# Ranks and edge lookups for the later chunks made during the first aggregation instead of the second, in a four-layer graph network on one core

## The reference

```python
def _sage_conv(x, src, dst, Wl, Wr, b):
    agg = jax.ops.segment_sum(x[src], dst, num_segments=n)
    deg = jax.ops.segment_sum(jnp.ones_like(dst, dtype=x.dtype), dst, num_segments=n)
    mean = agg / jnp.maximum(deg, 1.0)[:, None]
    return mean @ Wl + x @ Wr + b
...
h = jnp.maximum(_layernorm(x, axis=-1), 0.0)
h = relu(_sage_conv(h, ..., 1)); h = relu(_sage_conv(h, ..., 2)); h = relu(_sage_conv(h, ..., 3))
return x + _sage_conv(h, ..., 4)
```

## Time and profile before

| what | us |
|---|---|
| median of 3 runs | 749.73 (749.73 to 757.46) |
| profiled execution: its own time | 750.45 |
| profiled execution: span from first to last instruction | 748.7 |
| PE busy within the span | 675.0 (90%) |
| DVE busy | 289.1 (39%) |
| ACT busy | 172.8 (23%) |
| POOL busy | 31.3 (4%) |

### The profile page before, as it was taken

One profiled execution on the slowest core, in us unless ns is written; L12 is line 12 of the kernel. 1 busy time (PEld: TensorE's weight loads), 2 busy tenths in 40 slices (PEclk: granted clock), 3 DMA queues, 4 the chain that ended last, 5 costly groups with the idle time before them and its releaser, 6 DMA issues.

```text
span 748.7 us, 11542 instructions
## 1 busy us (share of the span) xinstructions
PE 675.0 (90%) x4545; PEld 367.8 (49%) x4546; DVE 289.1 (39%) x826; ACT 172.8 (23%) x339; POOL 31.3 (4%) x80
## 2 busy tenths in 40 slices
PE   5567867799999999999968999899999999999997
PEld 4234533566555555654434444444444646466464
DVE  6985864468477585840111222202221101001001
ACT  4755521345262361311100101102111000000000
POOL 3000030000000000000000000000000110110100
PEclk9998988979999999999989999999999999999999
DMA  8000200310010101034342334223325330230230
GB/s 259 13 1 1 88 1 31 127 33 5 9 50 16 56 16 32 27 17 57 116 127 80 100 111 153 93 67 114 112 108 208 102 106 12 86 99 3 95 98 28
DMA packets 39424, 53.50 MB, mean 71 GB/s; under 512 B 8557, under 2 KB 21518, under 8 KB 39376
## 3 DMA queue, kind: packets, MB, share of 16 engines
q1 hardware_dynamic: 39260, 52.59, 22.9%
q10 hardware_dynamic: 116, 0.24, 0.1%
HBM read 31.86 MB, written 20.97 MB: 71 GB/s over the span
## 4 chain that ended last, share of the span: by engine, by line
PE 80%; DVE 9%; ACT 3%; DMA 3%; issue 2%; POOL 1%; SPq 1%; DVEq 0%; ACTq 0%; POOLq 0%
PE agg_ps L1673 37%; PE window_ps L1673 12%; PE lin_ps L1641 10%; PE window_ps L1571 6%; PE lin_ps L1625 6%; DVE early L1121 3%; PE lin_ps L1692 2%; PE window_ps L1502 2%; PE turn_ps L1660 2%; PE lin_ps L1649 1%; ACT counts L1347 1%; DMA H_d<-newH 1%; DMA W<-in_L_gnn_Wr_dram 1%; ACT counts L1312 1%; PE turn_ps L1548 1%
## 5 line engine op out<-in xcount | busy, mean ns | idle before, releaser
L1673 PE MATMUL agg_ps<-counts,H 128*128 128x512 f16 (+2 forms) x1500 | 358.2, 372 | 6.4 <-DVE newH L1203 3.1
L1673 PEld LDWEIGHTS agg_ps<-counts,H 128*128 128x128 f16 x1500 | 129.9, 99 | 123.7 <-issue 12.7
L1121 DVE TENSOR_TENSOR early<-early 128x512 f16<-128x512 bf16 (+2 forms) x466 | 150.4, 388 | 48.2 <-PE window_ps L1571 46.2
L1347 ACT ACTIVATE counts<-window_ps 128x400 f16<-128x400 f32 x196 | 96.8, 504 | 119.7 <-PE window_ps L1571 114.8
L1571 PE MATMUL window_ps<-early 128*128 128x100 f16 (+1 forms) x892 | 99.2, 223 | 24.8 <-DVE early L1121 15.6
L1571 PEld LDWEIGHTS window_ps<-early 128*128 128x128 f16 x892 | 66.8, 100 | 100.3 <-ACT counts L1347 31.7
L1673 PE MATMUL window_ps<-counts,H 128*128 (+1 forms) x600 | 96.3, 316 | 0.0
L1673 PEld LDWEIGHTS window_ps<-counts,H 128*128 128x128 f16 x600 | 45.7, 98 | 49.6 <-issue 4.1
L1175 DVE SCALAR_TENSOR_TENSOR aggT<-agg_ps,columns,rdeg 128x512 f32<-128x512 f32 (+1 forms) x30 | 20.6, 715 | 95.9 <-PE agg_ps L1673 80.1
L814 POOL TENSOR_TENSOR newH<-newH,early 128x256 f32<-128x256 f32 (+1 forms) x25 | 17.3, 725 | 611.5 <-DMA newH<-in_x_dram 611.5
L1386 ACT ACTIVATE newT<-lin_ps,columns 128x512 f32<-128x512 f32 (+1 forms) x28 | 17.3, 632 | 107.9 <-PE lin_ps L1641 107.9
(11 more groups left out here) (152 smaller groups left out, 383.9 us busy)
## 6 DMA issues: line engine op xcount, KB each, us to landing
selfT<-hT_d SPq DMA_DIRECT2D x18, 512.0 KB, 4.3
hT_d<-newT SPq DMA_DIRECT2D x12, 512.0 KB, 4.2
rdeg<-rdeg_d SPq DMA_DIRECT2D x18, 256.0 KB, 4.5
...
```

Source lines behind the costliest of these rows:

```text
L1121: last = v.tensor_tensor(hot[:, group % GROUPS, 0:n * size].rearrange("p (r n d) -> p r n d", r=n, d=2), numbers_to[:, 0:size].rearrange(" ...
L1347: a.activation(counts[:, :, 2 * w * WIN:2 * (w + 1) * WIN].rearrange("p t (a w) -> p a t w", a=2), window_ps[:, FILL_AT[w] % 2, 0:2 * KEYS ...
L1673: last = m((agg_ps, window_ps)[bank][:, h, 0:n], H_of[:, k, part, h * P:(h + 1) * P], counts[:, k, chunk_cols(c, n)], start=first and part ...
```

## The change

Nothing is computed differently; work is issued elsewhere.

1. **Ranks.** `below` stands at the start of the first aggregation (`q` = 0), and PE sums at `k` = 2 of it (`RANK_K`), into `degree_ps`. Before, both stood in the second.
2. **Lookups.** `choose_late` is cut in four parts of four comparisons for each piece, and `bases` goes by piece; the eight parts stand between one-hots at `k` = 7 to 18 of the first aggregation. `select_rows` stands at `k` = 13 and 19 of it (`SELECT_K`), and both `late_tables` at 16 and 22.
3. **Norm.** Of the norm of chunk 3 the moments come behind the last steps ahead of the first aggregation and the rest is moved into it, and everything of chunk 2 too; the relus of the last three chunks on ACT are issued in halves, two tiles at a time.
4. **Bounds and short plan.** `bound_h1`, `bound_h2`, `plan_low` and `bound_h3` stand at `k` = 0, 2, 3 and 4 of the second aggregation. The three `squares` use three PSUM banks and no longer wait for the norms of the one before.
5. **Turns.** The four late `h0_turn` stand at `k` = 1, 4, 7 and 10 of the second aggregation and alternate between two pairs of PSUM banks.
6. **Scratch.** The tables of the lookups lie in `aggT`, `newT`, `partsT` and other rows of `counts`; POOL makes the keys without waiting for the scales.
7. **Map.** The eight products of `lin` and the two of `narrow` become events of the script, and in aggregations 3 to 5 each counts as two places (`LIN_SLOTS`) among which the steps are spread. In the second aggregation the products go four at `k` = 2 and four at `k` = 5.

```diff
+        work = []
+        for k in range(NT):
+            work += [("sum", k)]
+            if q == 1 and k in FIRST_LIN_K:
+                work += [("lin", 4 * FIRST_LIN_K.index(k) + j) for j in range(4)]
+            if q > 1 and k == LIN_K:
+                work += [("lin", j) for j in range(8)]
+            if q >= 1 and k == (FIRST_NARROW_K if q == 1 else NARROW_K):
+                work += [("narrow", j) for j in range(2)]
+            work += [("half", k)]
+        slots = [1 if kind in ("sum", "half") else LIN_SLOTS * (q != 2) for kind, _ in work]
...
+    LIN_K, NARROW_K, TURN_K = 2, 10, 18
+    FIRST_LIN_K, FIRST_NARROW_K = (2, 5), 13
+    LIN_SLOTS = 2
...
-        win_key_late = [row(9 + i, CH + (1 - i) * 2 * LATE_N, 2 * LATE_N).bitcast(f32) for i in range(2)]
+        win_key_late = [flat_new[:, i * LATE_N:(i + 1) * LATE_N] for i in range(2)]
...
-        SELECT_K = (8, 14)
-        H0_LATE_K = (4, 9, 12, 16)
-        RANK_K = 3
+        SELECT_K = (13, 19)
+        H0_LATE_K = (1, 4, 7, 10)
+        RANK_K = 2
...
-            pool.wait_ge(scales_made, 1)
...
-            def choose_late(piece):
+            def choose_late(piece, part):
                 a, b = PIECES[piece]
-                for g in range(RG):
+                if part == 0:
+                    if piece == 2:
+                        dve.wait_ge(lo_made, 3)
+                    bases(piece, base_late[piece - 2], a)
+                for g in range(part * RG // 4, (part + 1) * RG // 4):
...
-            first_round = {0: lambda: (h0_low_part(3), h0_shift(4)), 1: lambda: (degrees(0), h0_moments(5)),
...
-            second_round = {2: lambda: (bases((2, 3), base_late, NEXT), choose_late(2), choose_late(3)),
-                            8: lambda: late_tables(2), 13: lambda: low_part(1, 0, 0), 15: lambda: late_tables(3),
-                            20: lambda: copy_turned(1, 0, 0), 23: plan_low}
+            first_round = {0: lambda: (h0_shift(3), below(), degrees(0)), 1: lambda: h0_moments(4),
...
+            second_round = {0: bound_h1, 2: bound_h2, 3: plan_low, 4: bound_h3, 15: lambda: low_part(1, 0, 0),
+                            20: lambda: copy_turned(1, 0, 0)}
             for q in range(NCH):
-                if q == 1:
-                    below()
...
-                if i > 0:
-                    pe.wait_ge(norms_made, i)
+                if i == 1:
+                    pe.wait_ge(degree_inverted, 1)
                 for j in range(2):
                     for k in range(halves):
-                        last = m(turn_bank[:, j * width:(j + 1) * width], ones32,
+                        last = m(square_ps(i)[:, j * width:(j + 1) * width], ones32,
...
+            def lin_part(q, j):
+
+                n, t = size_of(chunk_at(q))
+                if j == 0:
+                    pe.wait_ge(agg_scaled[1], 2 * (q + 1))
+                    pe.wait_ge(self_loaded[1], 16 * (q + 1))
+                h, i = j // 4, j % 4
+                last = m(lin_ps[:, h, 0:n], W14[:, i // 2, i % 2, h * P:(h + 1) * P],
+                         (aggT, selfT)[i // 2][:, i % 2, 0:n], start=(i == 0), stop=(i == 3))
+                if i == 3:
+                    last.then_inc(lin_done[1], 1)
```

167 lines of the change are left out of this document (93 added, 74 removed).

## The result

The changed kernel takes 732.72 us in the median of 4 runs (732.22 to 734.05), the kernel before 750.37 (4 runs beside them): ratio 0.9751, 95% interval 0.9712 to 0.979. The profiled execution took 732.57 us with a span of 730.5, against 750.45 and 748.7: 18.2 us less between first and last instruction. The changed kernel came a second time later, beside its variants, and gave 732.84 (5 runs) and 0.977 (0.9748 to 0.9792). Forecast were 727 and a range of 718 to 737.

A forecast was written before the change was run, and what follows sets the result against it. PE was taken as the bound from the third aggregation on, with time to be had in layer 1 before; terms -2.0 + 6.5 - 25.7 - 0.5 - 1.5 = -23.2 from 750.45 gave 727 us, range 718 to 737.

The forecast's parts named there:

- the case as walked: The forecast's main case for the whole kernel: 727 us, own range 722 to 731, chance 0.54.
- the first aggregation costs more: Rival: DVE and PE alternate in waiting, so that stage takes 64 to 69 us, total 730 to 736; chance 0.2.
- First aggregation, +6.5: Layer 1's first aggregation grows by 6.5 us from 13.2 us of added PE work; bounds +3.3 and +9.5.
- a sign of being wrong: The prediction counts as wrong if the first aggregation takes more than 66 us.
- the walk between floor and ceiling: First aggregation: stepping through PE's and DVE's queues gave 59 to 61 us, between 57.6 (PE only bound) and 63.8.
- Second aggregation, -25.7: Layer 1's second aggregation shrinks from 50.2 to 24.5 us as rank sums, lookups and stalls leave; bounds -29 and -20.
- All four stalls: PE's long waits in the second aggregation, 3.06, 5.01, 1.52 and 4.29 us, 13.9 together, all said to go.
- Build, -2.0: Ahead of the first aggregation, one shift and one moments set leave DVE's queue: -2.0 us, bounds 0 and -3.7.
- Third aggregation, -0.5: Its half-clock start shortens as the stall before it goes but small matmuls stay: -0.5 us, bounds 0 and -2.1.
- Steps between map products, -1.5: Fourth to sixth aggregations: DVE works through the map, closing PE holes after it: -1.5 us, bounds 0 and -4.1.
- the bounds' chain: Rival: DVE's bounds wait on ACT's square roots, second aggregation takes 29 to 30 us, total 731 to 733; chance 0.08.
- the best case: Rival: PE's work alone in two aggregations, full clock, map holes closed: 716, half of that way 721; chance 0.14.

## Why the prediction was right, and where it was off

**It held in its range, by its rival.** 732.6 for the profiled execution is outside the 722 to 731 of the case as walked and inside the 730 to 736 of "the first aggregation costs more", which had 0.2. Direction, stages and mechanism came as said; the two large terms of the sum were mis-sized in opposite directions, by 3.7 and 3.2 us. That they nearly cancel, and that the median lies within 6 us of 727, is luck.

**First aggregation, +6.5, came as +10.2 (bound +9.5).** In the cut of the prediction, up to the last step, it took 64.7 us: more than the 60.8 as walked and less than the 66 that it named as a sign of being wrong. PE's added work was right (13.15 against 13.2), and so was DVE's total (52.2 in this cut, 51.9 said for one that is 1.6 us shorter). The step that failed is the walk between floor and ceiling, "I walked both queues and got 59 to 61 us". It took half of the idle time for room. The comparison of totals, 51.9 of DVE against 57.6 of PE, says which engine is the bound and nothing of the holes: these are made by single blocks, moments with a low part (2.7 us), ACT's halves and copies (2.9 in five), late tables (0.9), each longer than the ring or the two banks last, and moved PE work, which comes in blocks of its own, does not lie in them. That the new blocks of DVE do not matter by volume, and their place does, is shown by the two runs on DVE: 5.2 us less of comparisons gave 0.6, one set of moments two places earlier 3.8. The rival named moments and choose parts alike as holes; the runs show it of the moments, and of the choose parts only for the 0.5 us that one wait lost when three quarters of them were left out. Nor does a set of moments make a hole wherever it stands: two places earlier it added no wait.

**Second aggregation, -25.7, came as -28.9.** All four stalls went, as listed; the small waits in their place came to 2.4 us, 2.7 had been taken. The rest, 2.9, is the clock. The sum kept 18.9 us of PE work at the pace that it had before, the first four map matmuls at 3.39 us among it, and put +1.2 on top "since PE waits 1.7 us at its start as before": 20.1 us. PE waited 1.56 us there, and yet the clock stayed full and the work took 17.2 us. In the second profile of the same kernel it did not stay, the work took 20.2 and the stage 22.5, as the sum had it (22.8 in this cut). Over the ten profiles of this stage the mean is 20.5, so the forecast for it was 2.2 us too long on average.

**What of it gains, which the sum could not tell.** The prediction priced rank sums, lookups and stalls as separate items. Moving the ranks alone gave 8.4 of the 17.6 us, at a price of 0.9 us in the first aggregation, because the stall ahead of the first lookup hung on the ranks' copy and not on the lookup's own place. Moving the lookups shifted 10 us of PE work from one stage to the other: relative to the ranks alone, the first aggregation is 9.4 us longer and the second 16.4 shorter, of which 4.3 are the plan's stall and 1.5 the wait for the last transpose. The rest of the net is the plan (0 to 4.5, by the two runs), and the spread of the steps (2.2 to 2.7). No run moves the lookups alone: what these differences leave for it, 16.4 - 4.3 - 1.5 - 9.4 = 1.2 us, is arithmetic over two profiles and not shown, and no more than the scatter of the second stage.

**Halved relus, costed at nothing, without a word on the cover.** Whole, they take 7.0 us. That is their worth within the changed kernel; in the kernel before, with less work on PE, it was not measured. It is the largest error of method in the prediction: an edit that it did not price at all carries more than the difference of all terms together.

**Build, -2.0, came as -1.2, and as -0.8 over profiles.** Three profiles of before's program up to there start the first aggregation at 45.9 to 46.2 us, nine of the changed one at 44.9 to 46.0 (45.3 on average). The moved 3.8 us of DVE were in part a wait: DVE stood 1.5 us for ACT's high part instead of 0.3 before.

**Third aggregation, -0.5, came as +0.3.** The stage before it ran at a granted clock of 1.00, and yet the clock fell within the block of 100 small matmuls, 0.6 us behind its start, and stayed low until 138, source pairs at 1.0 us (last row of the timeline above):

```profile
131.40:138.00 6.60, 6.23 (x102) 3.97 (x99) 3.86 (x14) 1.29 (x3) 0.00 (x0) 0.50 0.12 42
```

The stall that had preceded it was gone, so the fall does not need the stall. By the Trainium skill, page "TensorE: Matmul & The Clock Gate", section "What's actually happening", activity releases the low clock; of the two readings weighed, the strict one for the stall would have taken 2.1 us and the trace disagrees, while the one that left the term at none agrees.

**Steps between map products, -1.5, came as -0.6 in the profile and -2.2 to -2.7 over the runs.** The profile of before happened to have the fewest falls of clock of the four without the spread. PE's idle time in the three, 4.1 us before and said to become 2.5, came as 3.2: what the steps did to the holes is 0.5 to 0.9 us, and the rest of the term is PE's pace, which the prediction did not have.

**POOL, 0.** Its keys lay beside DVE's first tables, and there the largest comparison took 1.13 us, against 1.12 in the kernel before; one cast of 0.23 took 0.42, and no other operation got longer by 0.1. The rule of the Trainium skill on the shared port (page "GPSIMD Engine Reference", section "Architecture") has no price here beyond the 0.2 us of that cast, for which the trace shows no cause. **The rest, 0, came as +1.9.** No instruction changed; over all profiles with all degrees it lies between 420.0 and 424.7, and that of before was among the lowest.

The other rivals did not come: the bounds' chain had 2.9 us to spare, the clock did come back, and the best case failed on the first aggregation's holes.
